# New memory layouts for Z, k, inverse, queries and Y in a delta-rule language-model layer, with merged transfers and inverse loads issued earlier

## The reference, cut to what matters

```python
T = jnp.tril(Bi @ KiT, k=-1)
inv = jnp.linalg.inv(eyeC + T)
Ui = inv @ (Vi - Bi @ W_t)
W_new = W_t + KiT @ Ui
...
O_i = Qi @ W_avg * a + Qi @ W_t * c + T_mat * (Qi @ KiT) @ Ui
```

## Time and profile before

| | |
|---|---|
| median of 3 runs | 1510.67 us (1509.09 to 1511.9) |
| the profiled execution | 1518.6 us, its span 1516.8 us |
| busy in the span | PE 1179.7 us, DVE 764.9, ACT 515.8, POOL 388.6 |
| transfers | 237366 packets, 228.68 MB, 151 GB/s on average |
| SP's transfer queue q1 | 202944 packets, 194.28 MB, 45.3% of the 16 engines' time |

### The profile page before, as it was taken

One profiled execution on the slowest core, in us unless ns is written; L12 is line 12 of the kernel. 1 busy time (PEld: TensorE's weight loads), 2 busy tenths in 40 slices (PEclk: granted clock), 3 DMA queues, 4 the chain that ended last, 5 costly groups with the idle time before them and its releaser, 6 DMA issues. The chain is left out here.

```text
span 1516.8 us, 28805 instructions
## 1 busy us (share of the span) xinstructions
PE 1179.7 (78%) x10846; PEld 791.1 (52%) x10846; DVE 764.9 (50%) x1707; ACT 515.8 (34%) x1049; POOL 388.6 (26%) x366
## 2 busy tenths in 40 slices
PE   4766456566656561688697987999999999999997
PEld 2543334353535351466475764555666666666664
DVE  4599849586868683567646873221111212121211
ACT  3454245353636360433243332331122222222221
POOL 6100113131202021513226003662022222222222
PEclk9788679777878785867888997999999999999999
DMA  7644566868585968777687747953122323232322
GB/s 269 188 101 134 120 178 142 251 140 248 128 255 121 259 136 235 199 224 224 179 246 225 230 152 278 377 171 103 32 40 46 48 45 49 44 49 43 49 44 31
DMA packets 237366, 228.68 MB, mean 151 GB/s; under 512 B 88980, under 2 KB 177972, under 8 KB 236080
## 3 DMA queue, kind: packets, MB, share of 16 engines
q1 hardware_dynamic: 202944, 194.28, 45.3%
q0 software_dynamic: 16368, 19.96, 7.5%
q10 hardware_dynamic: 17920, 12.59, 2.8%
HBM read 117.39 MB, written 115.62 MB: 154 GB/s over the span
## 5 line engine op out<-in xcount | busy, mean ns | idle before, releaser
L1644 DVE TENSOR_TENSOR hid_all<-p_s,silu 128x512 f32<-128x512 f32 x103 | 71.3, 692 | 378.8 <-PE p_s L1495 249.7
L1694 POOL DMA_INDIRECT out_h<-y_sb,x_in x71 | 110.6, 1558 | 360.9 <-DVE y_sb L1656 343.0
L1552 ACT ACTIVATE silu<-p_m 128x512 f32<-128x512 f32 x103 | 61.5, 597 | 328.0 <-PE p_m L1488 223.4
L804 DVE SCALAR_TENSOR_TENSOR cv<-raw,conv_sb,cv 128x512 f32<-128x512 f32 x144 | 117.5, 820 | 83.6 <-ACT raw L698 81.7
L175 DVE TENSOR_TENSOR xt<-xt,prod 128x62 f32<-128x62 f32 (+15 forms) x248 | 142.0, 572 | 4.3
L172 DVE TENSOR_TENSOR prod<-nx,xt 128x62 f32<-128x62 f32 (+15 forms) x248 | 138.4, 558 | 2.5
L1510 PE MATMUL p_y<-wo,hid_all 128*128 x568 | 134.4, 379 | 0.8 <-ACT hid_all L1569 0.8
L1488 PE MATMUL p_m<-wi,xT_c 128*128 x284 | 133.5, 592 | 0.5 <-ACT xT_c L1565 0.5
L1495 PE MATMUL p_s<-ws,xT_c 128*128 x284 | 133.6, 593 | 0.0
L288 PE MATMUL p_item<-xbd,bv_i 128*32 128x128 f32 x1024 | 46.8, 340 | 108.4 <-issue 39.5
L575 PE MATMUL p_p<-xT,wqkv_sb 128*128 128x512 f32 x192 | 108.6, 705 | 0.7 <-issue 0.7
(11 more groups left out here) (155 smaller groups left out, 2093.9 us busy)
## 6 DMA issues: line engine op xcount, KB each, us to landing
slots_in_dram<-xt SPq DMA_DIRECT2D x18, 520.0 KB
x_in<-slots_in_dram SPq DMA_DIRECT2D x71, 130.0 KB, 2.1
q_channels_dram<-qT SPq DMA_DIRECT2D x128, 64.0 KB
k_tokens_dram<-h SPq DMA_DIRECT2D x32, 256.0 KB
chunk_gram_dram<-h SPq DMA_DIRECT2D x32, 256.0 KB
beta_kv_dram<-h SPq DMA_DIRECT2D x8, 1024.0 KB
nx<-chunk_gram_dram SPq DMA_DIRECT2D x8, 1024.0 KB, 6.3
scores_dram<-h SPq DMA_DIRECT2D x8, 1024.0 KB
```

The lines of the kernel that those rows point to most:

```text
L804: ins = dve.scalar_tensor_tensor(cv[:, p, m, :], raw[:, p, m, j:j + L], conv_sb[:, p, m, j:j + 1], cv[:, p, m, :], ALU.mult, ALU.add)
L1644: dve.tensor_tensor(dst, p_s[n % 2][:], silu[n % 2][:], ALU.mult).then_inc(S["hid_ready"], 1)
L1694: pool.indirect_dma_start(token_rows, bass.IndirectOffsetOnAxis(x_in[s % X_IN][:, D:D + 1].bitcast(U32), 0), y_sb[s % 2][:], None, compute ...
```

## The change

Memory tensors that were laid out by chunk are laid out by sequence and token; Y and queries become one tensor, stored by one transfer per item and loaded by one per step. The inverse is stored as it lies in `xt`, by one transfer, and read in pieces of 256 B. Per sequence the stores of q go from 16 transfers to 8, of k from 4 to 1, of the inverse from 8 to 1; per item those of Z from 4 to 1 and of Y and queries from 2 to 1; per step the loads from 4 to 3. `load_x(r + 5)` stands in front of the wait for the Gram stores, and `store_item`, which takes the place of `store_y` and `store_rest`, comes later for Y.

```diff
-    x_dram = nc.dram_tensor("chunk_inverse_dram", [B, L, H * C], F32, kind="Internal").ap()
+    x_dram = nc.dram_tensor("chunk_inverse_dram", [B, HP, NC_BATCH, C, ROW], F32, kind="Internal").ap()
-    qT_dram = nc.dram_tensor("q_channels_dram", [B, TILES, P, HQ, P], F32, kind="Internal").ap()
-    kk_dram = nc.dram_tensor("k_tokens_dram", [NC_BATCH, B, C, 2 * D], F32, kind="Internal").ap()
-    y_dram = nc.dram_tensor("y_channels_dram", [B // GROUP, NC_BATCH, P, GROUP, HQ * C], F32, kind="Internal").ap()
-    qy_dram = nc.dram_tensor("queries_dram", [B // GROUP, NC_BATCH, P, GROUP, HQ * C], F32, kind="Internal").ap()
-    zo_dram = nc.dram_tensor("z_and_inner_dram", [NC_BATCH, B, C, 2 * D], F32, kind="Internal").ap()
+    qT_dram = nc.dram_tensor("q_channels_dram", [B, HQ, P, L], F32, kind="Internal").ap()
+    kk_dram = nc.dram_tensor("k_tokens_dram", [B, L, 2 * D], F32, kind="Internal").ap()
+    yq_dram = nc.dram_tensor("y_and_queries_dram", [B // GROUP, NC_BATCH, P, GROUP, 2 * HQ * C], F32, kind="Internal").ap()
+    zo_dram = nc.dram_tensor("z_and_inner_dram", [B, L, 2 * D], F32, kind="Internal").ap()
...
         def store_inverse(sp, b):
             sp.wait_ge(s_inv, b + 1)
-            for g in range(HP):
-                sp.dma_start(x_dram[b, :, g * ROW:(g + 1) * ROW].rearrange("(c k) x -> c k x", k=C),
-                             xt[b % 2][g * NC_BATCH:(g + 1) * NC_BATCH].rearrange("p k e i -> p k (e i)")
-                             ).then_inc(s_xst, 16)
+            sp.dma_start(x_dram[b].rearrange("g c k x -> (g c) (k x)"),
+                         xt[b % 2][:].rearrange("p k e i -> p (k e i)")).then_inc(s_xst, 16)
...
-                sp.dma_start(xbd[tok(c), c].rearrange("p h i -> p (h i)"), x_dram[b, t * P + c * C:t * P + (c + 1) * C]
+                sp.dma_start(xbd[tok(c), c].rearrange("p h i -> p (h i)"), x_dram[b, :, t * CH + c].rearrange("g k x -> k g x")
                              ).then_inc(s_x_in, 16)
...
+            sp.dma_start(q_i[:], qT_dram[b, :, :, t * P:(t + 1) * P].rearrange("n p l -> p n l")).then_inc(s_q_in, 16)
+
+        def store_item(sp, r):
             b, t, i = r // TILES, r % TILES, r % 2
             sp.wait_ge(T["z_ready"], r + 1)
             sp.wait_ge(T["inner_ready"], r + 1)
+            sp.dma_start(zo_dram[b, t * P:(t + 1) * P], zo_out[i][:].rearrange("p w h d -> p (w h d)")).then_inc(s_zo_st[i], 16)
+            sp.wait_ge(T["y_ready"], r + 1)
             sp.wait_ge(T["q_ready"], r + 1)
+            sp.dma_start(yq_dram[b // GROUP, t * CH:(t + 1) * CH, :, b % GROUP].rearrange("c p x -> p c x"),
+                         yq_out[i][:].rearrange("p c w n i -> p c (w n i)")).then_inc(s_yq_st[i], 16)
...
             if r >= 2:
-                act.wait_ge(s_y_st[r % 2], 16 * (r // 2))
+                act.wait_ge(s_yq_st[r % 2], 16 * (r // 2))
...
                         if b >= AHEAD:
-                            move_item(sp, r)
-                            move_item(sp, r + 1)
+                            load_scores(sp, r + 1)
+                            load_x(sp, r + 2)
+                            store_item(sp, r)
+                            load_scores(sp, r + 2)
                         if b >= 2:
                             store_inverse(sp, b - 2)
                         if b >= AHEAD:
-                            move_item(sp, r + 2)
+                            load_x(sp, r + 3)
+                            store_item(sp, r + 1)
+                            load_scores(sp, r + 3)
                         sp.wait_ge(s_nrm, b * 4 + 4)
...
+                        for n in range(HQ):
+                            for w in range(2):
+                                sp.dma_start(qT_dram[b, n].rearrange("(f w d) l -> w f d l", w=2, d=DH)[w],
+                                             qT[n % 2 * 4 * DH:(n % 2 + 1) * 4 * DH, n // 2]).then_inc(s_st, 16)
...
+                        sp.dma_start(kk_dram[b].rearrange("(t p) x -> p t x", p=P),
+                                     kk[:].rearrange("p t h w d -> p t (h w d)")).then_inc(s_st, 16)
...
                                 if b >= AHEAD:
-                                    move_item(sp, r + 3)
+                                    load_x(sp, r + 4)
+                                    store_item(sp, r + 2)
+                                    load_scores(sp, r + 4)
+                        if AHEAD <= b + 1 < B and b >= AHEAD:
+                            load_x(sp, r + 5)
                         sp.wait_ge(s_ngst, 64 * (b + 1))
...
+                        if AHEAD <= b < B - 1:
+                            store_item(sp, r + 3)
                         if b == AHEAD - 1:
                             load_x(sp, 0)
                             load_scores(sp, 0)
+                            load_x(sp, 1)
...
+                        if c % CH == 0:
+                            sp.wait_ge(s_zo_st[t % 2], 16 * done)
+                            sp.wait_ge(s_yq_st[t % 2], 16 * done)
                         if s >= 2:
                             sp.wait_ge(S["u_summed"], s - 1)
+                            sp.wait_ge(S["o_summed"], s - 1)
...
+                            sp.dma_start(yq[i][:].rearrange("p b w n i -> p (b w n i)"), yq_dram[g, c].rearrange("p b x -> p (b x)")
+                                         ).then_inc(s_yq[i], 16)
+                        sp.dma_start(zo[i][:].rearrange("p w d -> p (w d)"), zo_dram[b:b + GROUP, c * C:(c + 1) * C]
+                                     ).then_inc(s_zo[i], 16)
...
+                                         kk_dram[b:b + GROUP, c * C:(c + 1) * C]).then_inc(s_kk[i], 16)
```

More of the change, by code:

```diff
@@ L196, in build @@
         yz_ch = sb(tail, "yz_ch", [P, HQ, P])
-        y_out = [sb(tail, f"y_out{i}", [P, CH, HQ, C]) for i in range(2)]
+        yq_out = [sb(tail, f"yq_out{i}", [P, CH, 2, HQ, C]) for i in range(2)]
         yz_tok = sb(tail, "yz_tok", [P, H, 2 * DH])
@@ L201, in build @@
         sy_out = [sb(tail, f"sy_out{i}", [P, CH, HQ, C]) for i in range(2)]
-        qy_out = [sb(tail, f"qy_out{i}", [P, CH, HQ, C]) for i in range(2)]
         s_st = tail.enter_context(nc.semaphore("kv_stored"))
@@ L206, in build @@
         s_s_in = tail.enter_context(nc.semaphore("item_scores_loaded"))
-        s_bv_in, s_y_st, s_zo_st, s_qy_st = ([tail.enter_context(nc.semaphore(f"{n}{i}")) for i in range(2)]
-                                                     for n in ("item_bv_loaded", "y_stored", "zo_stored", "queries_stored"))
+        s_bv_in, s_zo_st, s_yq_st = ([tail.enter_context(nc.semaphore(f"{n}{i}")) for i in range(2)]
+                                                     for n in ("item_bv_loaded", "zo_stored", "y_queries_stored"))
         T = {n: tail.enter_context(nc.semaphore("item_" + n)) for n in (
@@ L249, in store_rest @@
             sp.wait_ge(T["inner_ready"], r + 1)
-            for c in range(CH):
-                sp.dma_start(zo_dram[t * CH + c, b], zo_out[i][tok(c)].rearrange("p w h d -> p (w h d)")
-                             ).then_inc(s_zo_st[i], 16)
+            sp.dma_start(zo_dram[b, t * P:(t + 1) * P], zo_out[i][:].rearrange("p w h d -> p (w h d)")).then_inc(s_zo_st[i], 16)
+            sp.wait_ge(T["y_ready"], r + 1)
             sp.wait_ge(T["q_ready"], r + 1)
[L254 to L264, removed]
+            sp.dma_start(yq_dram[b // GROUP, t * CH:(t + 1) * CH, :, b % GROUP].rearrange("c p x -> p c x"),
+                         yq_out[i][:].rearrange("p c w n i -> p c (w n i)")).then_inc(s_yq_st[i], 16)
         def sum_queries(pool, r):
@@ L275, in sum_queries @@
             pool.wait_ge(T["sy_ready"], r + 1)
-            pool.tensor_tensor(qy_out[i][:], qy_out[i][:], sy_out[i][:], ALU.add).then_inc(T["q_ready"], 1)
+            pool.tensor_tensor(yq_out[i][:, :, 1], yq_out[i][:, :, 1], sy_out[i][:], ALU.add).then_inc(T["q_ready"], 1)
         def apply_inverse(pe, r, bank, alone):
@@ L930, in build @@
             s_lane = [sem(ctx, f"b_embedded_lanes{i}") for i in range(4)]
-            s_yy, s_qq, s_zo, s_kk, s_xn_out, s_xnT_out = (
+            s_yq, s_zo, s_kk, s_xn_out, s_xnT_out = (
                 [sem(ctx, f"b_{n}{i}") for i in range(2)]
-                for n in ("y_loaded", "q_loaded", "zo_loaded", "kk_loaded", "xn_stored", "xnT_stored"))
+                for n in ("yq_loaded", "zo_loaded", "kk_loaded", "xn_stored", "xnT_stored"))
             S = {n: sem(ctx, "b_" + n) for n in (
@@ L998, in _ @@
                             r = item_in[s - 1]
-                            move_item(sp, r, more=r + 1 < ITEMS and r != BREAK)
+                            more = r + 1 < ITEMS and r != BREAK
+                            if more:
+                                load_x(sp, r + 1)
+                            store_item(sp, r - 1)
+                            if more:
+                                load_scores(sp, r + 1)
                         if s == 11:
@@ L1004, in _ @@
                         if s == step_of[ITEMS - 1] + 2:
```

(2 more changed lines are left out.)

55 lines of the change are left out of this document (12 added, 43 removed).

## The result

The changed kernel takes 1532.21 us, median of 4 runs (1522.0 to 1536.63), beside 1509.92 for the kernel before on the same chip. The ratio is 1.0136, 95% interval 1.0084 to 1.0189: slower by 1.4%. The profiled execution took 1530.76 us, its span 1529.0. What follows takes the two profiles apart, so it is about the 12.2.

The account below looks back on a forecast made before the run. Waits were taken to set stage A's pace and PE to bound stage B's full-clock scan. Terms -20 - 4 - 3 + 27 + 5 + 8 + 0 + 4 + 2 + 5 - 4 = +20 gave 1531 us, range 1488 to 1560.

Parts of the forecast that it names:

- Division over four engines: Loads of zo and kk_b and stores of q run on engines 0 to 3, 2.85 us a load; q1 173304 packets.
- Even spread, 1473: Rival, chance 0.16: transfers go over 16 engines in spite of the blocks; -38 us in all, 1473.
- Steps 20 to 30, +27: Scan in stage B, 11 steps: four engines become the bound, 8.3 us a step over 5.82; bounds 20, 38.
- What PE waits for there: In the scan's steps at full length, PE should be waiting for zo or kk_b.
- Steps 16 to 19, +5: Scan in stage B: steps 8.35 us long become 9.2 to 11 on four engines; bounds 4, 10.
- Steps 12 to 15, +8: Scan steps with items, stage B: 10.55 us long become 11.9 to 13.6 on four engines; bounds 5, 12.
- Second inverse store, -4: Stage B: the second time eight store commands (8.83 us) become one of about 0.4, saving 4 us; bounds -6, 0.
- Second items, -20: Stage A, four sequences: inverse loaded before the Gram wait, partly offset by the combined store; 4 x 5 us; bounds -31.4, 0.
- First items, -4: Stage A, first sequence: SP no longer 3.7 us late with the bv store holding the inverse load; bounds 0, -8.
- +5 for the queries' stores: Stage A: q stores on four engines make first items' loads land some 1.3 us later, four times; bounds 0, 10.
- Stage A gains all, 1495: Rival, chance 0.16: four engines, but the combined store lands in time, stage A -43, stage B +27; -16, 1495.
- the wait changes its name, 1551: Rival, chance 0.18: combined store lands as late as the inverse did; stage A keeps -4 - 3; +40, 1551.

Follow-up runs that it names:

- e2: Changed kernel, memory layout kept, each load of zo and kk_b issued as four commands of 32 rows: 1497.08 us, 0.9867.
- e1: Changed kernel with Z and k in their memory layout of before, four stores each, loads as one run of 128 rows: 1495.15 us, 0.9872.
- e4: Kernel before with one unused row between the blocks of Z and k in memory, so their loads have four blocks: 1545.52 us, 1.0203.
- e9: e2 with e3's edit, so split loads and the combined store moved forward: 1485.61 us, 0.9803.
- e10: e9 with e6's edit, so also the queries' layout and 16 stores of the kernel before: 1484.4 us, 0.9794.
- e6: Changed kernel with only the queries' layout and 16 stores of the kernel before: 1531.76 us, 1.0104.
- e8: Kernel before with the second item's inverse loaded in front of the Gram wait, layouts and commands kept: 1500.21 us, 0.9903.
- e12: Kernel before with the second item's inverse and scores both loaded in front of the Gram wait: 1493.4 us, 0.9921.
- e11: e10 with the second item's scores also loaded right behind its inverse, in front of the Gram wait: 1478.17 us, 0.9814.
- e3: Changed kernel with the combined store of a sequence's last item moved in front of the inverse load and Gram wait: 1520.93 us, 1.0026.

## Why the prediction was right, and where its steps were not

The time was forecast at 1531 and is 1532.21. That it fits to 1 us is luck: the terms are differences between profiles and add up to +20, the two profiles differ by 12.2, and the rest of the fit comes from the profile of before lying 7.9 above its median. Two large terms of opposite sign carried it, and both came near: stages before the barrier -19.6 where the terms gave -22 (-20, -4, -3, +5), stage B +33.3 where they gave +42 (27 + 5 + 8 + 0 + 4 + 2 - 4). So the mechanism stands and stage B is over-priced by 9, which is hardly more than stage B's scatter. The fairest price is after against e2, which differ in the division of the stage B loads alone: 36.4 us from barrier to stage C, where those terms gave 46 (27 + 5 + 8 + 0 + 4 + 2).

- **Division over four engines: right.** The packets match to the last one in the changed kernel and in e1, e2, e4, e9 and e10, each worked out ahead, and in e6 (175096), counted afterwards in the same way: 4 ends for a command over four blocks and 16 for one over 16, 32 or 128 rows. e4 puts the cost into the kernel before, e2 takes it out of the changed one without touching the layout. The pieces with a DMA share of 0.26 at 99 GB/s show that it is four engines that move the data. The Trainium skill, DMA: Bandwidth & Descriptors, "Why a DMA increments its semaphore by 16 and not by 1", has the engines as the largest number up to 16 that divides the slowest dimension of both sides, and every count here agrees with it. That it is the lowest-numbered engines no view here shows.
- **Even spread, 1473: wrong** as a description of this kernel. e2, where the loads are spread and nothing else is changed, is what it describes: 0.987, about half of the gain that it gave (0.975). e9 and e10, where the store is moved as well, reach 0.980.
- **Steps 20 to 30, +27: too much.** They measured +21, 7.76 us a step against 8.3. I counted 22 loads at 2.85 us; 19 fall into the 11 steps, and by engine time they are 3.25 each, which makes nearly the same 62 us. With the remainder of 19 + 9 that is 90 us or 8.2 a step. Where only the four are busy their 99 GB/s give 2.6 us a load, and with that price it would be 7.1 a step. The measured 7.76 lies between, so the sum came near, and its price is only as good as the crowding that it assumes.
- **What PE waits for there: wrong.** I expected `zo` or `kk_b`. It was ACT's store of `xnT`, and the step was slower by PE's clock as well: 73.63 us busy for the 1233 instructions that took 61.32 in e2. `zo` is what PE waits for at other steps: 3.5 us in steps 5 to 8, 11.76 in front of step 12 and 3.6 in steps 16 to 19.
- **Steps 16 to 19, +5: +3.7** (37.2 against 33.45; by my own price of 2.85 the term should have been 6). **Steps 12 to 15, +8: +5.6** (47.7 against 42.1). **Steps 5 to 8, 0: -2.2. Steps 0 to 3, +4: -1.6.** Only the 5.6 is well clear of the scatter: steps 16 to 19 take 33.45, 31.3 and 26.8 us in before, e8 and e12, which have the same stage B. At 0 to 3 the cheaper store of the inverse may be in it. **First load, +2:** from barrier to scan 9.2 us instead of 5.5, +3.7.
- **Second inverse store, -4: did not come.** The steps 9 to 11 took 35.2 us instead of 32.6, and the wait for `zo` that ends them is 11.76 us, which was 9.67 before. SP's timeline of the changed kernel:

```profile
719.80 0.32 SPq L182 DMA_DIRECT2D chunk_inverse_dram<-xt  x1
728.92 1.95 SPq L221 DMA_DIRECT2D xbd<-chunk_inverse_dram  x4
...
734.52 0.53 SPq L967 DMA_DIRECT2D zo<-z_and_inner_dram  x1
```

The store is issued in 0.32 us instead of 8.83, but the load behind it waits until it has landed: 9.1 us from the store's issue to the load's, where the eight commands took 11.9 (737.84 to 749.75). So `zo` was issued only 2.3 us sooner after the store (14.7 us instead of 17.0), and PE started on it 8.6 us after its issue instead of 3.7. The first is what the term was worth; the second is the division over four engines, which I had not counted at this step. In e1, e2, e9, e10 and e11, with the one store and the loads over 16 engines, the steps 9 to 11 take 29.1 to 31.5 us; in e3 and e6, whose loads lie on four, 32.5 and 34.0.
- **Second items, -20: right.** From the store of `bv` to the second item's L310 (L290 after) the kernel before took 33.9, 33.8, 33.9 and 32.0 us in its four sequences, the changed one 27.6, 28.6, 27.6 and 28.4: 21.4 less. Of that 3.7 is in front of the first item, which leaves 17.7. The store that ACT waits for let it go 12.05 us behind `nx` (507.70 - 495.65); I had taken 11.3. That the new wait is this store, e3 shows.
- **First items, -4: right; +5 for the queries' stores: wrong.** From the store of `bv` to PE's first item: 9.3, 7.6, 8.1, 7.5 us before, 7.2, 7.45, 7.1, 7.0 after, 3.7 less. The -4 was made for the first sequence only: there, from DVE's end to the first item, it was 11.1 us and is 7.25, 3.8 less, of which 1.8 are the store of `bv` itself, no longer late. The other three, which I had put at nothing, gave 1.6. e6 and e10 show that q's stores cost nothing there. That the wait in front of the line fell by 19.1 (38.5 to 19.4) is mostly not time gained: PE does other work in it.
- **End of stage A, -3: -1.9** (from the last store of `bv` to the barrier 24.9 and 23.0 us).
- **Missed in stage A:** the first store of `bv` comes 2.6 us earlier (261.37 instead of 263.93; 1.8 of them belong to the -4, and DVE was done 0.8 sooner), and 6.3 us are given back between the second items and the next store of `bv`: the four times from one such store to the next sum to 308.3 and 293.1, 15.1 less, not 21.4. PE's wait for DVE's `h` in line 629 (617 after) grew by 6.2 us (16.3 to 22.5), and in e8, which gives 6.0 back, to 21.8; no run took it apart. All together: -2.6 - 3.7 - 17.7 + 6.3 - 1.9 = -19.6. The +5 that did not come and the 6.3 that I had not seen hid each other: that the stages before the barrier came out at -19.6 against -22 is in part luck.
- **Stage A gains all, 1495; the wait changes its name, 1551:** neither. The wait did change its name, as the third rival says, but only for two thirds of its length (20.4 of 31.4 us).

## What to carry to other kernels

Before merging transfers, look at the outermost count on both sides of each command: a load of `[b, i]` blocks from memory into 128 partitions had 4, ran on four of 16 engines, and cost this kernel 2.7% (1.0136 against 0.9867), while the mean DMA share of the steps that it slowed fell. Keep such a layout if it saves stores elsewhere, but issue its load as one command per block: e2 and e9 have the cheap stores and the evenly spread loads, and e9 to e11 run 1.9 to 2.1% faster than the kernel before. And when two results share one store, the earlier one inherits the place in the queue of the later: put that store ahead of whatever the queue waits for next.

## What the runs showed that I had not expected

Transfers on four engines slowed small stores of another queue: ACT's 128 KB stores of `xnT` were waited for 0.7 us in the scan's steps 20 to 30 of the kernel before, and 12.7 us in the changed one. The one issued at 849.69 let ACT go at 858.17, 8.5 us later; in the kernel before the one issued at 839.47 had landed when ACT came for the buffer, 5.2 us later. A likely reason is that a store over 16 engines is done only when its share on the four full ones is; this was argued, not shown.

A bound on four engines looks like spare capacity: the DMA share of the stretch fell from 0.68 to 0.52 as the engines became the limit. It also lowered PE's granted clock, from 1.00 to 0.86, in a stretch where PE's idle share rose from 4% to 14%. The 0.86 is a mean: pieces of the stretch, 862 to 866 us for one, are at 0.50, the level of 1.2 GHz, and the others at 1.00, that of 2.4 GHz. The piece around 862 us began while PE stood idle 1.97 us for ACT, around 858 us. So some of the 21 us are PE running slower: its busy time grew by 12.1 us, its idle time by 9.1. In e2, where only the division of the loads is taken back, the clock is at 1.00 again.
